# Two-layer cross-attention and expert model on one core: the fullest of the last five second experts is worked last, and the end waits for tiles that hold rows

## The chip, the cores and the metric

The kernel runs on one core of one Trainium2 chip. The metric is the time of one execution on the device, in microseconds (us). Before the change the median of three runs is 881.79 us (879.25 to 882.55).

## The reference

The input is 16 items of 128 rows by 256 features, 2048 rows in all, and a context of the same shape. Two layers follow each other, each an attention over the context and a mixture of experts, both added to the rows with a gain. The part that matters here is the second mixture. Its eight experts are three-layer networks of width 256, 512, 512, 256, and each row goes to the two experts with the highest gate:

```python
gate_logits = jnp.einsum('bsd,dn->bsn', x, Wg) + bg
gate_weights = jax.nn.softmax(gate_logits, axis=-1)
topv, topi = jax.lax.top_k(gate_weights, TOPK)
h = jax.nn.gelu(jnp.einsum('bsd,ndh->nbsh', x, W1) + b1[:, None, None, :], approximate=False)
h = jax.nn.gelu(jnp.einsum('nbsh,nhf->nbsf', h, W2) + b2[:, None, None, :], approximate=False)
eo = jnp.einsum('nbsf,nfd->nbsd', h, W3) + b3[:, None, None, :]
comb = jnp.sum(jax.nn.one_hot(topi, NE, dtype=x.dtype) * topv[..., None], axis=-2)
out = jnp.einsum('nbsd,bsn->bsd', eo, comb)
```

The first mixture has 16 smaller experts and a shared one, and the same routing by two.

## The kernel before, in words

The five engines each have an instruction stream written out by hand; they meet through counting semaphores. The kernel has four stages. Stage A works through the 16 items in groups of four: first attention, shared expert, first routing. Stage B works 47 tiles of 128 rows through the first experts. Stage C (`c_turn` on VectorE, `item_turns`) goes item by item through the second attention and, two items at a time, through the second routing; VectorE keeps in `cnt` how many rows each expert has got so far, computes the slot of each row, and POOL scatters the normalised rows by indirect DMA into `xg1`, one region per expert. The pairs are routed at even turns, the last one (items 14 and 15) at turn 18, and `cnt` then gets its last sum.

`tables` (lines 746 to 821) runs on VectorE once after stage A and once after stage C. From the counts it makes the number of tiles of each expert (at least one for a second expert), their running sum `end`, and for each of the 39 second tiles (`NT1`) a row of `tab`: its expert, its first row in `xg1` and the place of its weights in a ring of three. Tiles past the last with rows get the last expert and the first row of `xg1`, and are computed like the others. It also makes `endi` (the ends, as integers), the two slots of each row in the tile order (`yslot`), sorted so that slot 0 is the lower one, and the number of stores of each parity after which all experts but the last are stored (lines 808 to 810). Before the tiles can be loaded, SP and ScalarE each write zeros behind the rows of four experts (`zero_tails`, lines 300 to 308).

Stage D works the 39 tiles. SP loads a tile into one of four buffers (`load_tile`), TensorE turns it and computes three products in pieces of high and low parts (line 1793), with VectorE splitting each operand (lines 1217, 1219) and ScalarE applying the activation (line 1419). In turn t of `p_turn` TensorE does the third product of tile t-1, the first of tile t+2 and the second of tile t+1. The first product of a tile waits until the weights of its expert are split. VectorE adds the last bias at line 1238, once the store of the tile two places before has landed, and SP stores the tile at line 449 (`store_output`).

POOL brings the weights. `load_weights(e)` issues three DMAs of expert e into one of two raw buffers, and `split_weights(e)` splits them into a place of the ring with a cast (line 509) and a subtraction (line 514), once the expert three before it has no tile left (`endi`). After the last split POOL gathers. 16 indirect DMAs bring the lower slot of each item's rows into the raw buffer of odd experts, after the stores of all tiles of experts 0 to 6; 16 more bring the higher slot into the other buffer, after the stores of all 39 tiles:

```python
stores = pool.value_load(endi[0:1, E1:E1 + 1], min_val=0, max_val=NT1 // 2)
for b in range(2):
    pool.wait_ge(s[f"output_stored{b}"], stores * 16)
```

VectorE, behind its last tile, adds the 16 low rows and then, two items at a time, the high ones (line 1246), and SP, behind its last tile store, stores each pair of finished items (line 462).

Of the kernel before, what the change touches and what calls it, by code (L numbers as in the profile page):

```python
# [54 lines left out]
def flamingo_kernel(nc, x, ctx, g_xattn, g_ffn, theta_wT, theta_b, phi_wT, phi_b, g_wT, g_b, ln_gamma, ln_beta,  # L55
# [26 lines left out]
    with ExitStack() as es:  # L82
# [68 lines left out]
        tab = sb("tab", [1, NT0, 3], I32)  # L151
# [204 lines left out]
        def _(sp):  # L356
# [106 lines left out]
            sp.wait_ge(s["out_stored"], NGE * 16)  # L463


        @blk.gpsimd
        def _(pool):
# [23 lines left out]
            def load_weights(e):  # L491

                at, b = 0, raw_buffer(e)
                for W, k_ in ((W1, KD), (W2, KH), (W3, KH)):
                    size = k_ * W.shape[2]
                    pool.dma_start(raw[b][:, at:at + size].rearrange("p (k n) -> p k n", k=k_),
                                   W[e].rearrange("(k p) n -> p k n", p=P)).then_inc(s[f"raw_loaded{b}"], 16)
                    at += size
# [171 lines left out]
            for b in range(2):  # L670
                pool.wait_ge(s[f"output_stored{b}"], (NT1 + 1 - b) // 2 * 16)
# [7 lines left out]
        def _(dve):  # L679
# [65 lines left out]

            def tables(lk, E, NT):
# [12 lines left out]
                if E == E1:  # L759
# [5 lines left out]
                lk.then(v.tensor_tensor(le, iota_f[:, 0:E].unsqueeze(2).to_broadcast((P, E, E)),  # L765
                                        iota_f[:, 0:E].unsqueeze(1).to_broadcast((P, E, E)), ALU.is_ge))
                lk.then(v.tensor_tensor(le, le, nt.unsqueeze(1).to_broadcast((P, E, E)), ALU.mult))
# [6 lines left out]
                lk.then(v.tensor_reduce(tabf[:, 0:NT, 0], ge, AX, ALU.add))  # L774
                lk.then(v.tensor_scalar(tabf[:, 0:NT, 0], tabf[:, 0:NT, 0], float(E - 1), None, ALU.min))
# [4 lines left out]
                lk.then(v.tensor_scalar(tabf[:, 0:NT, 2], iota_f[:, 0:NT], end[:, E - 1:E], float(P), ALU.is_lt, ALU.mult))  # L780
# [4 lines left out]
                if E == E1:  # L785


                    times = (E1 + 1) // RING
                    over = big1[:, 0:times * NT].rearrange("p (m t) -> p m t", m=times)
                    v.tensor_scalar(tabf[:, 0:NT, 2], tabf[:, 0:NT, 0], 2.0, None, ALU.add)  # L790
                    for m_ in range(times):
                        i = v.tensor_scalar(over[:, m_, :], tabf[:, 0:NT, 0], float(RING * (m_ + 1) - 2), -float(RING), ALU.is_ge, ALU.mult)
# [252 lines left out]
            def c_turn(t, k):  # L1045
# [154 lines left out]
                if choice:  # L1200
                    assert lk.k == PAIR

            item_turns(dve, c_turn)
# [239 lines left out]
        def _(pe):  # L1443
# [443 lines left out]
```

## Time and profile before

| what | value |
|---|---|
| median of three runs | 881.79 us |
| lowest and highest run | 879.25 and 882.55 us |
| the profiled execution | 890.49 us, of which 888.8 us are the span of its records |
| granted TensorE clock over the span | 0.891 of full speed |
| TensorE busy | 705.9 us (79%) |
| VectorE busy | 504.9 us (57%) |
| ScalarE, GpSimd (POOL) busy | 334.3 and 345.8 us (38% and 39%) |

The profile is of one execution; times in it count from the start of its span. PE is TensorE's matmul, PEld its weight load, DVE is VectorE, ACT ScalarE, POOL GpSimd, and SP the engine that issues most DMAs; a q behind a name is its sequencer, which issues DMAs and waits. L1793 is line 1793 of the kernel. A tile name such as `R` or `Q` stands for the memory that several named views share: `wraw` and `R` are the two raw buffers, `Q` holds the input and output tiles of stage D. An arrow reads out<-in. The records of matmuls have modelled ends.

### The profile page before, as it was taken

To read this page: it belongs to the slowest core of one execution; us is meant where nothing else is said; L and a number is where in the kernel's file an instruction comes from. 1 tells how busy PE (TensorE), PEld (TensorE's weight loads), DVE (VectorE), ACT (ScalarE), POOL (GpSimd) and SP (SyncE) were. 2 spreads that over 40 slices of the span, in tenths; PEclk is the share of its full clock that TensorE was granted. 3 is DMA by queue.
4 is the path that set the end of the run, shared out by engine and by line. 5 is a ranking of instruction groups with operands and counts; after the bars stand their busy time and mean duration, and the time that the engine had idled before them with its cause. 6 is when DMAs were issued, how large, how long until landed. Compare 5 with 4: busy or idle time off the path is not lost.

```text
span 888.8 us, 16798 instructions
## 1 busy us (share of the span) xinstructions
PE 705.9 (79%) x3975; PEld 524.9 (59%) x3976; DVE 504.9 (57%) x1347; ACT 334.3 (38%) x861; POOL 345.8 (39%) x355
## 2 busy tenths in 40 slices
PE   4788888835788897888788884499999999999910
PEld 2655665423555545666565662278888888888710
DVE  2547677571233346888788854545555555555533
ACT  0221340301244462455545561144545444454400
POOL 6243544350222233224445333690093448000175
PEclk9958999576899998989999986599999999999955
DMA  8931221033533327877677701543134131110135
GB/s 225 351 115 48 96 70 48 13 135 112 177 118 118 118 72 151 146 130 136 130 149 145 139 32 42 181 150 126 35 125 141 41 130 35 41 35 24 41 115 165
DMA packets 71340, 97.92 MB, mean 110 GB/s; under 512 B 11265, under 2 KB 59745, under 8 KB 71169
## 3 DMA queue, kind: packets, MB, share of 16 engines
q1 hardware_dynamic: 52960, 47.28, 22.2%
q0 software_dynamic: 14944, 47.89, 17.1%
q10 hardware_dynamic: 3392, 2.23, 0.8%
q8 instruction: 20, 0.33, 0.2%
q14 instruction: 24, 0.19, 0.1%
HBM read 63.81 MB, written 33.29 MB: 109 GB/s over the span
## 4 chain that ended last, share of the span: by engine, by line
PE 56%; issue 16%; DMA 9%; DVE 7%; POOL 6%; SPq 3%; ACT 3%; DVEq 0%; POOLq 0%; ACTq 0%
PE ps L1793 23%; PE ps L1624 5%; PE ps L1820 4%; PE ps L1614 3%; PE ps L1695 3%; PE ps L1634 3%; DMA QK<-qscr 2%; PE ps L1544 2%; PE ps L1713 2%; PE ps L1687 2%; POOL R L674 2%; POOL wraw L668 2%; DMA yg<-Q 2%; POOL xg L647 1%; PE ps L1574 1%
## 5 line engine op out<-in xcount | busy, mean ns | idle before, releaser
L1793 PE MATMUL ps<-WR,Hap 128*128 x468 | 118.5, 402 | 3.7 <-DVE Hap L1219 3.7
L1066 DVE TENSOR_REDUCE mraw<-ps 128x2 f32<-128x512 f32 x128 | 86.9, 683 | 22.0 <-PE ps L1687 20.5
L1425 ACT COPY Q<-ps 128x512 f32<-128x512 f32 x78 | 45.7, 586 | 142.3 <-PE ps L1793 142.2
L1793 PEld LDWEIGHTS ps<-WR,Hap 128*128 128x128 f32 x468 | 86.1, 191 | 21.2 <-issue 4.4
L1384 ACT ACTIVATE Q<-ps 128x512 f32<-128x512 f32 x128 | 74.2, 601 | 61.7 <-PE ps L1695 28.2
L1687 PE MATMUL ps<-QK 96*128 96x256 f32 x256 | 62.3, 328 | 21.5 <-DVE mraw L1066 10.1
L1217 DVE CAST Hbp<-ps 128x512 fp32r<-128x512 f32 x39 | 27.0, 692 | 78.6 <-ACT ps L1419 78.6
L1614 PE MATMUL ps<-ident,Q 128*128 128x128 f32 x172 | 36.8, 297 | 43.6 <-DMA Q<-xg 33.6
L1713 PE MATMUL ps<-QK 128*128 128x256 f32 x256 | 64.4, 335 | 7.1 <-ACT Q L1384 4.7
L1793 PE MATMUL ps<-WR,Hbp 128*128 x468 | 66.5, 292 | 2.9 <-issue 2.9
L483 POOL TENSOR_SCALAR veps<-st 128x1 f32<-128x1 f32 (+1 forms) x40 | 10.3, 259 | 138.1 <-DVE st L1108 62.9
L1793 PE MATMUL ps<-WR,XTp 128*128 x234 | 62.7, 404 | 1.3 <-DVE XTp L1219 1.3
L327 POOL DMA_DIRECT2D yg<-Q x46 | 25.0, 543 | 99.1 <-ACT Q L1329 99.1
L1687 PEld LDWEIGHTS ps<-QK 96*128 96x128 f32 x256 | 42.9, 204 | 32.6 <-DVE mraw L1066 16.9
L1793 PEld LDWEIGHTS ps<-WR,Hbp 128*128 128x128 f32 x468 | 59.4, 193 | 3.3 <-issue 3.2
L1614 PEld LDWEIGHTS ps<-ident,Q 128*128 128x128 f32 x172 | 21.4, 146 | 66.9 <-issue 60.5
L1713 PEld LDWEIGHTS ps<-QK 128*128 128x128 f32 x256 | 41.2, 202 | 21.9 <-issue 13.7
L1624 PE MATMUL ps<-R,Q 128*128 x188 | 52.0, 401 | 0.3 <-issue 0.3
L1820 PE MATMUL ps<-ident,Q 128*128 128x128 f32 x312 | 48.5, 278 | 4.1 <-issue 3.7
L668 POOL DMA_INDIRECT wraw<-yg,yslot x16 | 15.4, 963 | 89.9 <-DMA yg<-Q 85.4
L509 POOL CAST WR<-wraw 128x1024 fp32r<-128x1024 f32 (+1 forms) x8 | 18.6, 2319 | 78.7 <-PE ps L1793 69.1
L1793 PEld LDWEIGHTS ps<-WR,XTp 128*128 128x128 f32 x234 | 42.7, 195 | 8.9 <-issue 1.6
(265 smaller groups left out, 1511.5 us busy)
## 6 DMA issues: line engine op xcount, KB each, us to landing
Q<-xg SPq DMA_DIRECT2D x86, 128.0 KB, 2.1
QK<-kscr SPq DMA_DIRECT2D x48, 128.0 KB
QK<-qscr SPq DMA_DIRECT2D x48, 128.0 KB
yg<-Q POOLq DMA_DIRECT2D x47, 128.0 KB, 2.0
wraw<-in_W POOLq DMA_DIRECT2D x10, 512.0 KB, 8.2
wraw<-in_W POOLq DMA_DIRECT2D x5, 1024.0 KB, 7.5
yg<-Q SPq DMA_DIRECT2D x39, 128.0 KB
qscr<-split SPq DMA_DIRECT2D x32, 128.0 KB, 2.1
```

The costliest lines, as they stand in the source:

```text
L668: pool.indirect_dma_start(gLow[:, j, :], None, yg1[:, :], bass.IndirectOffsetOnAxis(ap=yslot[:, j, 0:1], axis=0)).then_inc(s["low_gathered ...
L1066: v.tensor_reduce(mraw[:, b, h, :], ps[:, h % 2, :].rearrange("p (c l) -> p c l", c=2), AX, ALU.max).then_inc(s["s_max"], 1)
L1217: v.tensor_copy(parts[0], src).then_inc(s[copied], 1)
L1384: a.activation(PTb[:, h % 4].rearrange("p c q -> p (c q)"), ps[:, 2 + h % 2, :], ACT.Exp, scale=DH ** -0.5).then_inc(s["st_exp"], 1)
L1425: a.copy(pre, ps[:, bank, :]).then_inc(s[f"l1_h{which}_copied"], 1)
L1614: i = tr(ps[:, b, k * P:(k + 1) * P], Xin[:, x, k * P:(k + 1) * P], ident[:])
L1624: i = mm(ps[:, 2 + b, 0:2 * F0], XTt[:, b, k * P:(k + 1) * P], Wug[:, bass.ds(e, 1), k, :, :].rearrange("p x a f -> p (x a f)"), start=(k ...
L1634: mm(ps[:, 4 + b, 0:D], h0T[:, b, :], Wds[:, bass.ds(e, 1), :].rearrange("p a d -> p (a d)"), start=True, stop=True).then_inc(s["tile_y"], 1)
L1687: i = mm(ps[:, h % 2, c * D:(c + 1) * D], QS[0:NK, n, h, c * P:(c + 1) * P], KS[0:NK, n, h, :], start=True, stop=True)
L1713: i = mm(ps[:, 2 + h % 2, c * D:(c + 1) * D], KS[:, k, h, c * P:(c + 1) * P], QS[:, k, h, :], start=True, stop=True)
L1793: i = mm(out, parts(x_part, k), ring[:, bass.ds(place, 1), o:o + width].rearrange("p r n -> p (r n)"), start=(k == 0 and x_part == 0 and w ...
L1820: i = tr(ps[:, bank, f * P:(f + 1) * P], pre[:, f * P:(f + 1) * P], ident[:])
```

## The change

Three things change. At the end of turn 17 of stage C, when 14 of the 16 items are counted, VectorE computes an order of the second experts (`order_experts`): of experts 3 to 7 the one with most rows so far is moved to the last place, and those behind it move up by one. The tables count places instead of experts where order matters, `tab` gets a fourth column with the place, and POOL reads from `tail` which expert's weights to load for a place from 3 on. Last, the waits of the two rows of gathers: `tables` computes for each parity the number of stores up to the last place but one, and up to the last place, and POOL waits for these, so that the tiles past the last with rows are not waited for by POOL. Their computation and their stores stay.

```diff
@@ sync, at the end
             sp.wait_ge(s["out_stored"], NGE * 16)
+            for b in range(2):
+                sp.wait_ge(s[f"output_stored{b}"], (NT1 + 1 - b) // 2 * 16)
@@ load_weights
                 at, b = 0, raw_buffer(e)
+                which = e if e < RING else pool.value_load(tail[0:1, E1 + e:E1 + e + 1], min_val=0, max_val=E1 - 1)
                 for W, k_ in ((W1, KD), (W2, KH), (W3, KH)):
                     size = k_ * W.shape[2]
                     pool.dma_start(raw[b][:, at:at + size].rearrange("p (k n) -> p k n", k=k_),
-                                   W[e].rearrange("(k p) n -> p k n", p=P)).then_inc(s[f"raw_loaded{b}"], 16)
+                                   W[bass.ds(which, 1)].rearrange("o (k p) n -> p (o k) n", p=P)).then_inc(s[f"raw_loaded{b}"], 16)
@@ gpsimd, after the splits
-            stores = pool.value_load(endi[0:1, E1:E1 + 1], min_val=0, max_val=NT1 // 2)
-            for b in range(2):
-                pool.wait_ge(s[f"output_stored{b}"], stores * 16)
+            def tiles_stored(which):
+                at = E1 + 2 * which
+                stores = [pool.value_load(endi[0:1, at + b:at + b + 1], min_val=0, max_val=(NT1 + 1) // 2) for b in range(2)]
+                for b in range(2):
+                    pool.wait_ge(s[f"output_stored{b}"], stores[b] * 16)
+
+            tiles_stored(0)
             alone(pool)
...
-            for b in range(2):
-                pool.wait_ge(s[f"output_stored{b}"], (NT1 + 1 - b) // 2 * 16)
+            tiles_stored(1)
             alone(pool)
@@ vector, new
+            place_of_e = meta[:, 6, 0:E1]
+            last_e, up_by, down_by, place_end = (meta[:, 8, k:k + 1] for k in range(4))
+            behind, up_to = (r[:, 2:4].rearrange("p j k e -> p (j k e)").rearrange("p (e f) -> p e f", e=E1) for r in (ohx, oh))
+
+            def order_experts(lk):
+                E, n = E1, RING
+                scratch, chosen, ids = meta[:, 5, 0:E], meta[:, 7, 0:E], iota_f[:, 0:E]
+                lk.then(v.tensor_tensor(scratch, cnt[:, 0:E], base[E][:], ALU.subtract))
+                lk.then(v.scalar_tensor_tensor(scratch, scratch, float(2 * E), ids, ALU.mult, ALU.add))
+                lk.then(v.tensor_reduce(place_end, scratch[:, n:E], AX, ALU.max))
+                lk.then(v.tensor_scalar(chosen[:, n:E], scratch[:, n:E], place_end, None, ALU.is_equal))
+                lk.then(v.tensor_tensor(chosen[:, n:E], chosen[:, n:E], ids[:, n:E], ALU.mult))
+                lk.then(v.tensor_reduce(last_e, chosen[:, n:E], AX, ALU.add))
+                lk.mark(v.tensor_scalar(up_by, last_e, -1.0, float(E), ALU.mult, ALU.add))
+                lk.then(v.tensor_scalar(down_by, last_e, float(E), None, ALU.subtract))
+                beyond, moved = meta[:, 0, 0:E], meta[:, 1, 0:E]
+                lk.mark(v.tensor_scalar(beyond, ids, last_e, None, ALU.is_ge))
+                lk.mark(v.tensor_scalar(scratch, ids, last_e, up_by, ALU.is_equal, ALU.mult))
+                lk.then(v.tensor_scalar(chosen, ids, float(E - 1), down_by, ALU.is_equal, ALU.mult))
+                lk.mark(v.tensor_tensor(scratch, scratch, beyond, ALU.subtract))
+                lk.then(v.tensor_tensor(moved, chosen, beyond, ALU.add))
+                lk.mark(v.tensor_tensor(moved, moved, ids, ALU.add))
+                lk.then(v.tensor_tensor(place_of_e, scratch, ids, ALU.add))
+                lk.mark(v.tensor_copy(tail[0:1, E:2 * E], moved[0:1, :]))
+                at = place_of_e.unsqueeze(1).to_broadcast((P, E, E))
+                lk.mark(v.tensor_tensor(behind, place_of_e.unsqueeze(2).to_broadcast((P, E, E)), at, ALU.is_ge))
+                lk.then(v.tensor_tensor(up_to, ids.unsqueeze(2).to_broadcast((P, E, E)), at, ALU.is_ge))
@@ tables, where E == E1
+                    total = place_end
+                    lk.mark(v.tensor_reduce(total, nt, AX, ALU.add))
+                    lk.then(v.tensor_tensor(le, behind, nt.unsqueeze(1).to_broadcast((P, E, E)), ALU.mult))
...
+                    moved = big1[:, NT * E:NT * E + 2 * NT].rearrange("p (m t) -> p m t", m=2)
+                    lk.mark(v.tensor_scalar(moved[:, 0, :], tabf[:, 0:NT, 3], last_e, None, ALU.is_ge))
+                    lk.then(v.tensor_scalar(moved[:, 1, :], tabf[:, 0:NT, 3], float(E - 1), down_by, ALU.is_equal, ALU.mult))
+                    lk.then(v.tensor_tensor(moved[:, 0, :], moved[:, 0, :], moved[:, 1, :], ALU.add))
+                    lk.mark(v.tensor_tensor(tabf[:, 0:NT, 0], tabf[:, 0:NT, 3], moved[:, 0, :], ALU.add))
...
-                lk.then(v.tensor_copy(endi[0:1, 0:E], end[0:1, :]))
-                v.tensor_copy(tab[0:1, 0:NT, :], tabf[0:1, 0:NT, 0:3]).then_inc(s["table_ready"], 1)
+                n_col = 4 if E == E1 else 3
+                if E != E1:
+                    lk.then(v.tensor_copy(endi[0:1, 0:E], end[0:1, :]))
+                v.tensor_copy(tab[0:1, 0:NT, 0:n_col], tabf[0:1, 0:NT, 0:n_col]).then_inc(s["table_ready"], 1)
@@ tables, where E == E1, behind the table
-                    halves = tabf[:, 0:NT // 2, 3]
-                    lk.then(v.tensor_scalar(halves, iota_f[:, 0:NT // 2], 2.0, end[:, E - 2:E - 1], ALU.mult, ALU.is_lt))
-                    lk.then(v.tensor_reduce(meta[:, 5, 0:1], halves, AX, ALU.add))
-                    lk.then(v.tensor_copy(endi[0:1, E:E + 1], meta[0:1, 5, 0:1]))
+                    le = big1[:, 0:E * E].rearrange("p (e f) -> p e f", e=E)
+                    ends = meta[:, 5, 0:E]
+                    lk.then(v.tensor_tensor(le, up_to, nt.unsqueeze(1).to_broadcast((P, E, E)), ALU.mult))
+                    lk.then(v.tensor_reduce(ends, le, AX, ALU.add))
+                    n_half = (NT + 1) // 2
+                    halves = big1[:, 0:2 * n_half].rearrange("p (x i) -> p x i", x=2)
+                    for x in range(2):
+                        i = v.tensor_scalar(halves[:, x, :], iota_f[:, 0:n_half], 2.0, ends[:, E - 2 + x:E - 1 + x], ALU.mult, ALU.is_lt)
+                    lk.then(i)
+                    stores = meta[:, 5, E:E + 4].rearrange("p (x b) -> p x b", x=2)
+                    lk.then(v.tensor_reduce(stores[:, :, 0], halves, AX, ALU.add))
+                    lk.then(v.tensor_tensor(stores[:, :, 1], ends[:, E - 2:E], stores[:, :, 0], ALU.subtract))
+                    lk.then(v.tensor_copy(endi[0:1, 0:E + 4], meta[0:1, 5, 0:E + 4]))
@@ end of c_turn
+                if isinstance(t, int) and t == B + 1:
+                    order_experts(ll)
@@ p_turn
-                    e1, place1 = pe.value_load(tab[0:1, t + 2, 0:1], min_val=0, max_val=E1 - 1), place_of(t + 2)
+                    e1, place1 = pe.value_load(tab[0:1, t + 2, 3:4], min_val=0, max_val=E1 - 1), place_of(t + 2)
```

## Rows read from the trace of the kernel before

**Rows 1.** The page, the chain that ended last, by engine.

```profile
PE 56%; issue 16%; DMA 9%; DVE 7%; POOL 6%; SPq 3%; ACT 3%; DVEq 0%; POOLq 0%; ACTq 0%
```

**Rows 2.** The same chain in order of time, its end: start us, us, what.

```profile
829.60 2.83 PE ps L1793 x18
836.40 2.31 DMA yg<-Q
```

**Rows 3.** Timeline of POOL from 836: start us, us, engine, line, operation, count, idle before.

```profile
839.57 1.02 POOL L668 DMA_INDIRECT wraw<-yg,yslot  x1 [85.35 <-DMA yg<-Q]
...
859.86 0.96 POOL L674 DMA_INDIRECT R<-yg,yslot  x1 [0.31 <-issue]
...
862.38 1.03 POOL L674 DMA_INDIRECT R<-yg,yslot  x1 [0.30 <-issue]
...
865.30 3.26 POOL L674 DMA_INDIRECT R<-yg,yslot  x1 [0.31 <-issue]
...
881.67 0.96 POOL L674 DMA_INDIRECT R<-yg,yslot  x1 [0.30 <-issue]
```

**Rows 4.** Timeline of all engines from 836: VectorE, and TensorE's last product.

```profile
841.11 0.42 DVE L1238 TENSOR_TENSOR Q<-ps,b3bc 128x256 f32<-128x256 f32 x1 [0.15 <-issue]
...
846.81 2.92 PE L1793 MATMUL ps<-WR,Hbp 128*128 x12 [2.92 <-issue]
...
855.59 0.42 DVE L1238 TENSOR_TENSOR Q<-ps,b3bc 128x256 f32<-128x256 f32 x1 [8.38 <-remote]
...
861.30 6.42 DVE L1246 SCALAR_TENSOR_TENSOR xs<-wraw,wts,xs 128x256 f32<-128x256 f32 x16 [5.28 <-DMA wraw<-yg,yslot]
...
884.50 0.88 DVE L1246 SCALAR_TENSOR_TENSOR xs<-R,wts,xs 128x256 f32<-128x256 f32 x2 [1.64 <-DMA R<-yg,yslot]
```

**Rows 5.** Timeline of SP: the stores of tiles 26, 36 and 38.

```profile
776.18 0.36 SPq L449 DMA_DIRECT2D yg<-Q  x1
...
841.62 0.33 SPq L449 DMA_DIRECT2D yg<-Q  x1
...
856.11 0.33 SPq L449 DMA_DIRECT2D yg<-Q  x1
```

**Rows 6.** Timeline: POOL's splits for places 6 and 7, TensorE's first products of tiles 26, 27.

```profile
731.45 9.03 POOL L514 TENSOR_TENSOR WR<-R,WR 128x4096 fp32r<-128x4096 f32 x1 [0.18 <-POOL WR L509]
...
745.17 9.04 POOL L514 TENSOR_TENSOR WR<-wraw,WR 128x4096 fp32r<-128x4096 f32 x1 [0.18 <-POOL WR L509]
...
748.25 1.55 PE L1793 MATMUL ps<-WR,XTp 128*128 x6
...
755.00 1.55 PE L1793 MATMUL ps<-WR,XTp 128*128 x6
```

**Rows 7.** Timeline of VectorE: the last gate, the table, the slots, the first tile's cast.

```profile
549.44 0.17 DVE L1162 TENSOR_REDUCE lmx<-lb 128x2 f32<-128x16 f32 x1
549.65 0.17 DVE L1172 TENSOR_TENSOR ex<-lb,lmx 128x16 f32<-128x16 f32 x1
...
550.10 0.17 DVE L1076 TENSOR_REDUCE den<-ex 128x2 f32<-128x16 f32 x1 [0.28 <-ACT ex L1407]
...
561.13 0.27 DVE L797 CAST tab<-tabf 1x117 int32<-1x117 f32 x1
...
564.92 0.18 DVE L821 CAST yslot<-idxf 128x32 uint32<-128x32 f32 x1
...
566.03 0.42 DVE L1217 CAST XTp<-ps 128x256 fp32r<-128x256 f32 x1 [0.92 <-PE ps L1614]
```

**Rows 8.** The chain in order of time: the last zeroed tail and the first loaded tile.

```profile
560.56 1.70 DMA xg<-zeros
563.07 2.06 DMA Q<-xg
```

**Rows 9.** Windows: stretch, its length, busy us (count) of each engine, clock, DMA share, GB/s.

```profile
842.00:844.00 2.00, 1.89 (x17) 1.65 (x15) 0.00 (x0) 0.59 (x1) 1.49 (x2) 1.00 0.52 141
...
846.00:848.00 2.00, 1.19 (x5) 1.19 (x6) 1.08 (x2) 0.00 (x0) 1.70 (x2) 0.51 0.40 109
```

More of the change, by code:

```diff
@@ L150, in flamingo_kernel @@
         tabf = sb("tabf", [P, NT0, 4])
-        tab = sb("tab", [1, NT0, 3], I32)
+        tab = sb("tab", [1, NT0, 4], I32)
         endi = sb("endi", [1, E0], I32)
@@ L764, in tables @@
                 le = big1[:, 0:E * E].rearrange("p (e f) -> p e f", e=E)
-                lk.then(v.tensor_tensor(le, iota_f[:, 0:E].unsqueeze(2).to_broadcast((P, E, E)),
-                                        iota_f[:, 0:E].unsqueeze(1).to_broadcast((P, E, E)), ALU.is_ge))
-                lk.then(v.tensor_tensor(le, le, nt.unsqueeze(1).to_broadcast((P, E, E)), ALU.mult))
+                total = end[:, E - 1:E]
+                if E == E1:
+                    total = place_end
+                    lk.mark(v.tensor_reduce(total, nt, AX, ALU.add))
+                    lk.then(v.tensor_tensor(le, behind, nt.unsqueeze(1).to_broadcast((P, E, E)), ALU.mult))
+                else:
+                    lk.then(v.tensor_tensor(le, iota_f[:, 0:E].unsqueeze(2).to_broadcast((P, E, E)),
+                                            iota_f[:, 0:E].unsqueeze(1).to_broadcast((P, E, E)), ALU.is_ge))
+                    lk.then(v.tensor_tensor(le, le, nt.unsqueeze(1).to_broadcast((P, E, E)), ALU.mult))
                 lk.then(v.tensor_reduce(end, le, AX, ALU.add))
@@ L773, in tables @@
                                         end.unsqueeze(1).to_broadcast((P, NT, E)), ALU.is_ge))
-                lk.then(v.tensor_reduce(tabf[:, 0:NT, 0], ge, AX, ALU.add))
-                lk.then(v.tensor_scalar(tabf[:, 0:NT, 0], tabf[:, 0:NT, 0], float(E - 1), None, ALU.min))
+                at = 3 if E == E1 else 0
+                lk.then(v.tensor_reduce(tabf[:, 0:NT, at], ge, AX, ALU.add))
+                lk.then(v.tensor_scalar(tabf[:, 0:NT, at], tabf[:, 0:NT, at], float(E - 1), None, ALU.min))
+                if E == E1:
+                    moved = big1[:, NT * E:NT * E + 2 * NT].rearrange("p (m t) -> p m t", m=2)
[3 more added lines that the diff above has]
+                    lk.mark(v.tensor_tensor(tabf[:, 0:NT, 0], tabf[:, 0:NT, 3], moved[:, 0, :], ALU.add))
                 lk.then(v.tensor_tensor(ge, ge, nt.unsqueeze(1).to_broadcast((P, NT, E)), ALU.mult))
@@ L778, in tables @@
                 lk.then(v.tensor_tensor(tabf[:, 0:NT, 1], iota_f[:, 0:NT], tabf[:, 0:NT, 1], ALU.subtract))
-                lk.then(v.tensor_scalar(tabf[:, 0:NT, 2], iota_f[:, 0:NT], end[:, E - 1:E], float(P), ALU.is_lt, ALU.mult))
+                lk.then(v.tensor_scalar(tabf[:, 0:NT, 2], iota_f[:, 0:NT], total, float(P), ALU.is_lt, ALU.mult))
                 lk.then(v.tensor_tensor(tabf[:, 0:NT, 1], tabf[:, 0:NT, 1], tabf[:, 0:NT, 2], ALU.mult))
@@ L789, in tables @@
                     over = big1[:, 0:times * NT].rearrange("p (m t) -> p m t", m=times)
-                    v.tensor_scalar(tabf[:, 0:NT, 2], tabf[:, 0:NT, 0], 2.0, None, ALU.add)
+                    v.tensor_scalar(tabf[:, 0:NT, 2], tabf[:, 0:NT, 3], 2.0, None, ALU.add)
                     for m_ in range(times):
-                        i = v.tensor_scalar(over[:, m_, :], tabf[:, 0:NT, 0], float(RING * (m_ + 1) - 2), -float(RING), ALU.is_ge, ALU.mult)
+                        i = v.tensor_scalar(over[:, m_, :], tabf[:, 0:NT, 3], float(RING * (m_ + 1) - 2), -float(RING), ALU.is_ge, ALU.mult)
                     lk.then(i)
@@ L1201, in c_turn @@
                     assert lk.k == PAIR
+                if isinstance(t, int) and t == B + 1:
+                    order_experts(ll)
+            ll.before = NGA * LATE
+            ll.turn(0, 0)
             item_turns(dve, c_turn)
```

## The prediction

> **What bounds the kernel now.** I read the chain that ended last first. Over the whole span it is mostly TensorE [rows 1]; in order of time TensorE carries it through the tiles of the second experts until 836 us, then it passes to the store of one tile [rows 2] and to POOL. The reader should see what POOL does there: after 85 us of idleness it issues 32 indirect gathers, one every 1.26 us, from 839.57 to 882.63 [rows 3]. The next view, the timeline of the same stretch, shows what stands beside them: VectorE writes the output of tile 36 at 841.11 and of tile 38, the last, at 855.59, then adds the 16 low rows in 6.42 us from 861.30, and finishes the last high pair 0.88 us after 884.50 [rows 4]. So after 839.57 us the end is set by POOL's issue of gathers, not by tiles. The low gathers start there because they wait for the store of tile 35: experts 0 to 6 end at place 36. Running the reference's router over its inputs gives rows per expert 1077, 24, 797, 492, 8, 1205, 439, 54, that is 9, 1, 7, 4, 1, 10, 4, 1 tiles, 37 in all; tiles 37 and 38 are empty.
>
> **What the change removes.** Among experts 3 to 7 expert 5 has most rows, by so much that the two items not yet counted can't alter it. The order becomes 0, 1, 2, 3, 4, 6, 7, 5 and the places end at 9, 10, 17, 21, 22, 26, 27, 37 tiles. A token's lower slot then lies before tile 27, so the 16 low gathers wait for the store of tile 26, issued at 776.18 [rows 5], and end near 779.3 + 20.2 = 799.5 us, while tiles 29 and 30 run. That is the gain: 16 gathers, 859.86 - 839.57 = 20.3 us [rows 3], leave the chain.
>
> **What takes their place.** The high gathers now wait for the store of tile 36, not of 38. It is issued at 841.62 [rows 5]; a store lands in 2.31 us [rows 2], POOL starts 0.8 us later as it did at 839.57, so at 844.7 us. Sixteen gathers at 1.26 us end at 864.6 if nothing disturbs them. VectorE can't start its low adds before it has written tile 38, at 856.0 [rows 4], because they stand behind it in its queue. They then run from 856.0 to 862.4, beside the gathers. In the trace the three gathers begun from 862.38 to 865.30, beside such adds, took until 868.56, 6.2 us instead of 3.5 [rows 3]: 2.7 us lost. After the change the adds of high rows already gathered follow at once, so VectorE is busy for about 10.5 us without a break (6.4 for 16 low rows, some 4 for nine or ten high ones), against 8 in the trace. I take 3.7 us of loss; the ends are 2.7 and 4.7. The last gather ends at 864.6 + 3.7 = 868.3. From there to the end of the span the trace has 888.8 - 882.6 = 6.2 us (landing, last pair, last store). New end without costs: 874.5, a saving of 14.3 us. If the gathers lost nothing, VectorE itself would end its adds at 856.0 + 6.4 + 16 x 0.44 = 869.4, and 3.4 us of stores give 872.8; with 4.7 us it is 875.5. SP is no term: it stores tile 38 at about 856, before the first pair of rows is ready.
>
> The lock deserves a check. While VectorE added, three gathers were slowed, but they were not stopped for all of the 6.42 us [rows 3, 4].
>
> The Trainium skill (SBUF — State Buffer, Who interferes with whom) has VectorE and GpSimd share a port pair, and whichever comes second is blocked fully. By that rule the gathers could stand still for the whole burst of adds; the trace agrees in part only, with one gather of 3.26 us.
>
> **What the change adds.** (a) The order is computed on VectorE at the end of the turn before the last pair is routed: 18 small operations, 11 of them waited for. A small one steps by 0.21 us (549.44 to 549.65) [rows 7], so 11 x 0.21 = 2.3 for the waited ones, and an estimated half of that for each of the seven that are not, 0.7: 3.0 us. VectorE has only 0.3 us of idleness there, before 550.10 [rows 7]. Everything behind is a chain: the last pair's routing, the tails, the tables, the first tile. I charge 2.8 us, with ends 2.0 (some operations fall closer together) and 3.6. (b) The tables grow. Up to the table itself: four operations on 39 elements and a sum are added, a mask and a copy are removed, net 0.4 us. The table is ready at 561.4 [rows 7], but SP waits for the zeroed tails (560.56 + 1.70 = 562.26) and loads at 563.07 [rows 8]: covered; were that cover gone, it would cost 0.4. From the table to the slots: seven operations and a copy in place of three, about 0.8 us. VectorE is free 1.2 us later, at 566.3 instead of 565.1, and the first cast of a tile began at 566.03 [rows 7]: 0.3 us on the path. POOL's first split moves by 1.2 us too; its result is wanted nine tiles later, so nothing. (c) Register work: POOL reads one value for each of five weight loads, in a queue that idles for tens of microseconds between splits; TensorE, VectorE and SP read as many as before. Nothing.
>
> **(d) The weights' order.** This is where cover could fail. Place 7 is now needed for tile 27, not for tile 36. Its split can't start earlier, as the place whose buffer it takes still ends at tile 22: POOL finishes it at 745.17 + 9.04 = 754.21, and TensorE starts tile 27's first product at 755.00 [rows 6]. A margin of 0.8 us, so zero; each microsecond beyond costs one. Place 6 (split ended at 740.5) is wanted at 748.3: safe. I allow 0 to 1.5 us.
>
> **The sum**, against the profiled execution (890.49 us, of which 888.8 are span): -14.3 + 2.8 + 0.3 = -11.2 us. The median of the runs is 881.79, 8.7 below that execution, with runs from 879.25 to 882.55; I carry the difference over unscaled: 870.6 us. With the ends (872.8 or 875.5 for the tail, 2.3 or 5.4 of cost) the change lies between -13.7 and -7.9, so 868.1 to 873.9, and 1.5 us each way for the scatter of runs.
>
> **Rivals.**
> - **The adds stop the gathers.** If the port is held for the whole burst, POOL stands for 6.4 us and for each high row's add that is ready behind it, some nine, 3.8 us: 10.2 us lost instead of 3.7, so 870.6 + 6.5 = 877.1 us. For it: the 3.26 us gather. Against: gathers got through in that burst. By the Trainium skill's rule above the time would be this one. 8%.
> - **The end still waits for all tiles**, because the count of tiles with rows isn't what reaches POOL. Then the high gathers start after tile 38's store (issued 856.1 [rows 5], landed and seen 3.1 later), at 859.2, as now at 859.86: nothing gained, 2 to 3 us of cost, near 884 us. The arithmetic of the diff speaks against it. 3%.
> - **Slower: the low gathers hold up the tiles they now run beside.** Place: the wait of VectorE for the tile store two places back, and the products it feeds. For it: with the gathers running, tile 38's output came only after 8.4 us of idleness [rows 4], though TensorE began its last product at 846.81. If each of three tiles lost 6 us so, it would be 18 us, and 888.6 in all. It decides from 5.2 us a tile, (11.2 + 4.4) / 3. Against: from 842 to 844, with gathers moving 141 GB/s, TensorE was busy 1.89 of 2.00 us at full clock, and the slow output falls where the granted clock is 0.51, after a drained pipeline [rows 9]. 4%.
> - **A late place 7.** POOL's split is slowed or begun later; TensorE idles, and its clock may fall. 2 to 4 us, 873 to 875. 8%; it overlaps the main case's range.
>
> **How the numbers follow.** Main case 77%: 870.6, own range 866.6 to 875. The rivals have 8, 3, 4 and 8%. The range 866.5 to 877.3 takes in the late place and the lock and leaves out the two others and the tails. A measurement of this kernel can tell about 0.5%, 4.4 us, from no change: below 877.4 counts as faster. Main case, late place and a part of the lock (its 877.1 lies at the edge) give 0.87; the rest of it and the wait for all tiles, 0.08; the held-up tiles, 0.05.
>
> **What would show it.** Sixteen gathers into the first buffer near 779 to 800 us (plus the shift of 3), with TensorE's products at their old pace beside them; the second sixteen from some 4 us after tile 36's output, while the last tiles still run; a block of small VectorE operations of about 3 us after the gate of the last pair; POOL's last split ending just before tile 27's first product. The forecast is wrong if the low gathers appear only after tile 35, if the high ones start after tile 38's store, if TensorE waits at tile 27, or if a gap opens between the tiles at 780 to 805 us.

## The result, and the profile after

The change makes the kernel slower, by 1.0%. The kernel after has a median of 892.68 us (883.49 to 896.09, 5 runs), the kernel before 881.79 us (878.5 to 884.74, 5 runs of the same session): ratio 1.0097, 95% interval 1.0055 to 1.014. The forecast was 870.6 us. All ratios in this document leave out runs in the slow state (one of four of e4_extra, one of seven of e6_narrow, five of the 25 of before beside e1 to e4); the medians include them.

The profiled execution after took 883.49 us (span 881.9). It and that of before differ by 13 us before the changed code runs: the last gate's first operation is at 549.23 us before and at 536.09 after, a stretch whose length varies from run to run. So the two are compared from that operation on. From it to the end of the span: before 888.8 - 549.2 = 339.6 us, after 881.9 - 536.1 = 345.8 us, that is 6.2 more. In three stretches:

```
stretch                                          before   after    forecast
last gate to tile 0's first product               17.94    20.90    +3.1
tile 0's first product to tile 38's first        263.70   280.52     0
tile 38's first product to the end                57.93    44.39   -14.3
```

The first stretch is +2.96, the third -13.5: both as forecast. The middle one was to stay as it was and grew by 16.8 us.

The page of after, the chain that ended last, by engine (to [rows 1]):

```profile
PE 58%; DVE 12%; issue 9%; DMA 8%; POOL 4%; ACT 3%; another core or an unknown queue 2%; SPq 2%; DVEq 0%; POOLq 0%; ACTq 0%
```

POOL's share falls from 6 to 4%: the low gathers left the chain. "Another core or an unknown queue", 2% on a kernel of one core, is new. It is time for which the profile names no releaser: 16.64 and 1.68 us near 771 and 788 us, where the time went, and 2.89 us at 409.54, in the routing, beside a row of four scatters (406.65 to 411.58). Two of these pieces and the end of the same chain in order of time, start us, us, what (to [rows 2]):

```profile
771.27 16.64 another core or an unknown queue
...
788.46 1.68 another core or an unknown queue
...
847.76 0.43 DVE Q L1306
...
848.27 3.33 DMA yg<-Q
...
852.48 0.95 POOL R L681
...
859.23 3.65 POOL R L681
...
874.76 2.93 DMA R<-yg,yslot
```

Its end now runs through tile 36's output and store, as the change intends, and through 16 gathers, not 32. The timeline of POOL after, start us, us, engine, line, operation, count, idle before (to [rows 3] and [rows 6]):

```profile
733.60 9.02 POOL L517 TENSOR_TENSOR WR<-wraw,WR 128x4096 fp32r<-128x4096 f32 x1 [0.18 <-POOL WR L512]
767.25 1.02 POOL L676 DMA_INDIRECT wraw<-yg,yslot  x1 [24.62 <-DMA yg<-Q]
...
786.25 0.96 POOL L676 DMA_INDIRECT wraw<-yg,yslot  x1 [0.30 <-issue]
852.48 0.95 POOL L681 DMA_INDIRECT R<-yg,yslot  x1 [65.27 <-DMA yg<-Q]
```

The 16 low gathers go out in one row without a pause, one every 1.26 us, from 767.25 to 787.21. Now the timeline of TensorE in the same stretch:

```profile
743.37 1.55 PE L1861 MATMUL ps<-WR,XTp 128*128 x6
...
771.10 1.55 PE L1861 MATMUL ps<-WR,XTp 128*128 x6
...
773.06 3.01 PE L1861 MATMUL ps<-WR,Hap 128*128 x12
788.58 1.11 PE L1888 MATMUL ps<-ident,Q 128*128 128x128 f32 x4 [12.51 <-ACT Q L1493]
793.04 2.92 PE L1861 MATMUL ps<-WR,Hbp 128*128 x12 [3.35 <-DVE Hbp L1287]
795.76 2.38 PE L1861 MATMUL ps<-WR,XTp 128*128 x6
```

Tile 27's first product (743.37) comes 0.75 us after POOL's split for place 7 (733.60 + 9.02): in time. Tile 31 starts at 771.10, tile 32 only at 795.76, 24.66 us later, where a tile takes 6.7 to 7.4. TensorE waits for ScalarE and VectorE; what do they wait for? The timelines of ScalarE and VectorE:

```profile
787.94 0.58 ACT L1493 COPY Q<-ps 128x512 f32<-128x512 f32 x1 [16.66 <-remote]
```

```profile
772.03 0.69 DVE L1287 TENSOR_TENSOR Hap<-ps,Hap 128x512 fp32r<-128x512 f32 x1
791.47 0.69 DVE L1285 CAST Hbp<-ps 128x512 fp32r<-128x512 f32 x1 [18.75 <-ACT ps L1487]
```

The circle starts at ScalarE's copy at 787.94. It copies what TensorE's first products of tile 31 wrote, and by the modelled ends those were over at 772.65. "Remote" says that the profile found no releaser near the end of the wait. The trace file also holds the moment at which each semaphore is raised (no view prints it), and there the delay shows. XTp, Hap and Hbp are what the first, second and third product of a tile read:

```
product that signals                     modelled end   signal   late by
after: Hbp products just ahead of tile 31   771.26      779.44     8.18
after: first products of tile 31 (XTp)      772.65      787.91    15.27
after: the Hap products behind them         776.07      790.26    14.19
before: last products of tile 38 (Hbp)      849.74      855.46     5.72
```

ScalarE is released 0.03 us after the signal of 787.91, and that signal comes 0.7 us after the last gather's end at 787.21. The fourth row was in the trace of before all along: the 8.4 us of idleness ahead of tile 38's output [rows 4] end 0.13 us after this signal, with the low gathers under way beside it.

Were the products themselves late, or only their signals? The transposes that stand between those first products and the Hap products (modelled end 773.30) signal at 790.13, and the twelve Hap products behind them only 0.13 us later, at 790.26. The same two signals are 2.77 us apart where nothing is held (798.81 and 801.58). So most of the twelve products had run before the signal ahead of them was raised. The same pair comes 0.12 to 0.13 us apart in e4_extra, e6_narrow and e11_three_flying below. For the first products of tile 31 this can't be told.

Windows of the stretch: stretch, its length, busy us (count) of TensorE, its weight loads, VectorE, ScalarE, POOL, clock, DMA share, GB/s; after first, then e2_pairs, an experiment described below, in which nothing is held:

```profile
764.00:771.50 7.50, 7.50 (x47) 6.49 (x47) 4.46 (x9) 3.84 (x12) 3.34 (x4) 1.00 0.24 70
771.50:779.00 7.50, 4.57 (x23) 3.45 (x22) 1.19 (x2) 0.00 (x0) 5.67 (x7) 1.00 0.41 122
779.00:788.00 9.00, 0.00 (x0) 0.00 (x0) 0.00 (x0) 0.06 (x1) 6.38 (x7) 0.58 0.36 104
788.00:795.80 7.80, 3.87 (x17) 3.48 (x18) 3.65 (x7) 3.16 (x10) 0.00 (x0) 0.50 0.12 37
```

```profile
771.50:779.00 7.50, 7.50 (x45) 6.37 (x44) 3.94 (x7) 4.19 (x14) 3.91 (x4) 1.00 0.29 86
779.00:788.00 9.00, 8.63 (x49) 6.82 (x47) 5.66 (x11) 4.05 (x13) 1.94 (x3) 1.00 0.27 89
```

All engines but POOL fall silent together, and the DMA engines are at 0.36 to 0.41 of their time, so no transfer path is full on average. The granted clock falls from full to half (2.4 to 1.2 GHz) at 780.5, after TensorE's last recorded product has ended (776.07): so it can't be what stopped it. It stays at half until 797.6 and costs a little of what comes at 788 to 796.

The timeline of VectorE after, at the last gate and the tables (to [rows 7]) and at the end (to [rows 4]):

```profile
536.50 0.17 DVE L1236 TENSOR_TENSOR ex<-lb,lmx 128x16 f32<-128x16 f32 x1
536.59 0.16 DVE L763 TENSOR_TENSOR meta<-cnt,base 128x8 f32<-128x8 f32 x1
...
539.46 0.21 DVE L782 TENSOR_TENSOR oh<-iota_f,meta 128x64 f32<-128x64 f32 x1
539.70 0.17 DVE L1140 TENSOR_REDUCE den<-ex 128x2 f32<-128x16 f32 x1
...
555.76 0.18 DVE L885 CAST yslot<-idxf 128x32 uint32<-128x32 f32 x1
555.85 0.42 DVE L1285 CAST XTp<-ps 128x256 fp32r<-128x256 f32 x1
```

```profile
855.30 0.42 DVE L1306 TENSOR_TENSOR Q<-ps,b3bc 128x256 f32<-128x256 f32 x1 [1.42 <-issue]
855.64 6.42 DVE L1314 SCALAR_TENSOR_TENSOR xs<-wraw,wts,xs 128x256 f32<-128x256 f32 x16
862.09 1.67 DVE L1314 SCALAR_TENSOR_TENSOR xs<-R,wts,xs 128x256 f32<-128x256 f32 x4
...
877.72 0.88 DVE L1314 SCALAR_TENSOR_TENSOR xs<-R,wts,xs 128x256 f32<-128x256 f32 x2 [1.67 <-DMA R<-yg,yslot]
```

The order of the experts is worked out from 536.59 to 539.67, and den, the gate's next step, stands at 539.70, 3.20 us after ex where it was 0.45 us before: 2.75 for the order, against 2.8 charged.

### The profile page after: what moved, and what is told of

The parts are those of the page before. It is cut to its first block, busy times and chain, and to the rows that moved or that the text cites. A ratio compares the mean times of both kernels' runs of the same rounds, so it can differ in the third digit from the quotient of the medians.

```text
span 881.9 us, 16879 instructions
## 1 busy us (share of the span) xinstructions
PE 700.3 (79%) x3975; PEld 519.0 (59%) x3976; DVE 508.1 (58%) x1372; ACT 333.2 (38%) x861; POOL 347.7 (39%) x355
## 4 chain that ended last, share of the span: by engine, by line
PE 58%; DVE 12%; issue 9%; DMA 8%; POOL 4%; ACT 3%; another core or an unknown queue 2%; SPq 2%; DVEq 0%; POOLq 0%; ACTq 0%
PE ps L1861 24%; PE ps L1692 5%; PE ps L1888 4%; PE ps L1682 3%; PE ps L1702 3%; PE ps L1573 2%; PE ps L1763 2%; PE ps L1755 2%; PE ps L1642 2%; POOL R L681 2%; PE ps L1781 2%; DMA yg<-Q 2%; DVE mraw L1130 2%; PE ps L1612 1%
## 5 line engine op out<-in xcount | busy, mean ns | idle before, releaser
L1888 PE MATMUL ps<-ident,Q 128*128 128x128 f32 x312 | 48.9, 280 | 16.8 <-ACT Q L1493 12.8
L1682 PEld LDWEIGHTS ps<-ident,Q 128*128 128x128 f32 x172 | 21.3, 145 | 59.6 <-issue 53.7
L1888 PEld LDWEIGHTS ps<-ident,Q 128*128 128x128 f32 x312 | 35.4, 142 | 30.2 <-issue 15.9
```

The costliest lines, as they stand in the source:

```text
L1682: i = tr(ps[:, b, k * P:(k + 1) * P], Xin[:, x, k * P:(k + 1) * P], ident[:])
L1888: i = tr(ps[:, bank, f * P:(f + 1) * P], pre[:, f * P:(f + 1) * P], ident[:])
```

## The experiments

Two theories were set against each other first: a row of indirect gathers holds TensorE (its signals come late while POOL issues them), or something else in the change opens the gap. Diffs are against the kernel after, but for e4_extra.

**e1_low_late**: the low gathers wait for tile 35's store, as before the change (both semaphores at 18 stores); order, tables and the second wait stay changed.

```diff
             tiles_stored(0)
+            for b in range(2):
+                pool.wait_ge(s[f"output_stored{b}"], 18 * 16)
             alone(pool)
```

> The changed kernel with the new order kept, but its low gathers held until tile 35 is stored, as before the change. Theory G (indirect gathers hold TensorE back while POOL issues them): no gap between the first products of tiles 31 and 32, which are then 6.8 us apart instead of 24.7; the end as before the change, so 882 + 3 us of ordering = 885. Rival O (the new order itself stalls the tiles, by late weights): the gap of 18 us stays and the time is near 900.

Measured: 890.22 us (median of 10), ratio 1.0078 (1.0034 to 1.0122). The gap is gone: tile 32 starts 6.79 us after tile 31. So order and tables do not make the gap. But the time is not that of before plus 3. The timelines of VectorE, TensorE and POOL of e1_low_late near its end:

```profile
864.03 0.42 DVE L1308 TENSOR_TENSOR Q<-ps,b3bc 128x256 f32<-128x256 f32 x1 [14.51 <-remote]
```

```profile
849.11 2.92 PE L1863 MATMUL ps<-WR,Hbp 128*128 x12 [3.87 <-issue]
```

```profile
840.42 1.02 POOL L678 DMA_INDIRECT wraw<-yg,yslot  x1 [84.59 <-DMA yg<-Q]
...
860.71 0.95 POOL L683 DMA_INDIRECT R<-yg,yslot  x1 [0.30 <-issue]
861.96 0.96 POOL L683 DMA_INDIRECT R<-yg,yslot  x1 [0.31 <-issue]
```

The high gathers follow at 0.30 us, as they did before (859.86 [rows 3]), so the row is 32 long in both. Tile 38's last product (modelled end 852.03) signals at 863.89, 11.9 us late, and the low adds wait for that output. From tile 38's first product to the end it is 60.2 us, 57.9 before: the gain of the second part is eaten by a longer hold, which I had not expected. Why it is 11.9 us here and 5.7 before is not shown; here the signal came when the row still had 18 us to go.

**e2_pairs**: the low gathers go two at a time, each two behind the output of one more tile, from tile 26 on.

```diff
             for j in range(B):
+                if j % 2 == 0:
+                    pool.wait_ge(s["tile_out"], NT0 + 27 + j // 2)
+                    alone(pool)
                 pool.indirect_dma_start(gLow[:, j, :], None, yg1[:, :],
```

> The changed kernel with its 16 low gathers issued two at a time, one pair behind the output of each of tiles 26 to 33. If theory G holds in proportion (each gather costs TensorE about 1.1 us wherever it stands), the time stays near 892, with some 2 us lost in each of eight tiles. If TensorE is held only after several gathers on end (in the traces the delay set in 3 to 4 us after the first one), the tiles keep their 6.8 us and the time is 871 to 875.

Measured: 873.09 us (median of 10), ratio 0.9918 (0.9874 to 0.9962). The timeline of POOL of e2_pairs:

```profile
773.45 1.00 POOL L679 DMA_INDIRECT wraw<-yg,yslot  x1 [0.30 <-issue]
776.81 0.95 POOL L679 DMA_INDIRECT wraw<-yg,yslot  x1 [2.35 <-DVE Q L1309]
...
783.43 0.96 POOL L679 DMA_INDIRECT wraw<-yg,yslot  x1 [4.41 <-DVE Q L1309]
```

The same 16 gathers of the same rows, with tile steps of 6.7 to 7.4 us beside them. From the last gate to the end it takes 868.7 - 540.6 = 328.1 us, 11.5 less than before; my sum was -11.2. But 1.6 of the 11.5 is half clock in the trace of before, at 576 us, and not of the change: 9.9 are left, and the ratio's interval stands for 3.4 to 11.1. So most of the prediction's sum comes back once the row is broken up, and this kernel is faster than both.

**e3_plain**: in place of each low gather a plain transfer of as many bytes in the same queue.

```diff
-                pool.indirect_dma_start(gLow[:, j, :], None, yg1[:, :],
-                                        bass.IndirectOffsetOnAxis(ap=yslot[:, j, 0:1], axis=0)).then_inc(s["low_gathered"], 16)
+                pool.dma_start(gLow[:, j, :], yg1[j * P:(j + 1) * P, :]).then_inc(s["low_gathered"], 16)
```

> The changed kernel with 16 plain DMAs of 128 KB on POOL's queue in place of the 16 low gathers, from the first 16 tiles of the result; the low rows that are added are then others than the reference's. Rival T (traffic: 2 MB moved in a burst beside the tiles is what holds TensorE): the gap at tile 32 stays, 10 us or more. Theory G (it is the indirect form): no gap, time 870 to 876.

Measured: 871.5 us (median of 8), ratio 0.9899 (0.9848 to 0.995); tile 32 comes 6.87 us after tile 31. POOL issues the sixteen in 8.52 us, faster than the indirect ones, and holds nobody. Their row is shorter than 20 us, but eight indirect gathers in 9.9 us do hold TensorE (e9_eights below). Neither the bytes, nor the destination, nor a busy queue of POOL's is enough; the indirect form matters.

**e4_extra**: the kernel before, with 16 indirect gathers more (of other rows, into the same buffer, which the true gathers then overwrite) behind tile 26's store.

```diff
+            for b in range(2):
+                pool.wait_ge(s[f"output_stored{b}"], (14 - b) * 16)
+            alone(pool)
+            for j in range(B):
+                pool.indirect_dma_start(gLow[:, j, :], None, kscr.rearrange("a t d -> (a t) d"),
+                                        bass.IndirectOffsetOnAxis(ap=slotl[:, j % GA, j // 8:j // 8 + 1], axis=0)).then_inc(s["extra"], 16)
+            pool.wait_ge(s["extra"], B * 16)
...
+                    few = big1[:, 0:2 * GA].rearrange("p (j k) -> p j k", j=GA)
+                    lk.then(v.tensor_scalar(few, slotf[:, 0:GA, :], float(2 * TOK - 1), None, ALU.min))
+                    v.tensor_copy(slotl[:], few)
```

> The kernel before with 16 more indirect gathers, from another tensor into the first raw buffer, behind the store of tile 26; nothing of the change in it. Theory G: a gap of 15 to 20 us opens between the first products of tiles near 31, and the time is 897 to 904. Rival O: POOL is idle there, so nothing: 882 to 883.

Measured: 902.03 us (median of 4), ratio 1.0234 (1.0131 to 1.0338). Tile 32 comes 24.59 us after tile 31, and the wait is the known one, though the view puts it down to "issue" here. The timeline of ScalarE of e4_extra (its gathers went from 762.53 to 782.5):

```profile
780.41 0.58 ACT L1435 COPY Q<-ps 128x512 f32<-128x512 f32 x1 [13.82 <-issue]
785.53 1.11 ACT L1429 ACTIVATE ps<-ps,b2T 128x128 f32<-128x128 f32 x4 [4.53 <-remote]
```

So the hold needs nothing of the change: the row alone, put beside tiles of the old kernel, makes it.

**e5_fours**: as e2_pairs, in rows of four behind every second tile (the condition is `j % 4 == 0`).

> The changed kernel with its low gathers issued four at a time (5 us on end), every second tile. Theory G with an onset (TensorE is held only from about 3.5 us after the first of a row of gathers, until the row ends): about 1.5 us lost in each of four rows, gaps of 8 to 9 us between some first products of tiles 28 to 36, and a time of 876 to 880. If the loss is one for the row of sixteen alone, 873 as in pairs.

Measured: 872.29 us (median of 4), ratio 0.9875 (0.9822 to 0.9929). Four tile steps are a little long: 7.03, 7.37, 7.74 and 7.27 us where e2_pairs has 6.79, 6.75, 6.81 and 6.66, 2.4 us in all. The 876 to 880 us of the theory with an onset at 3.5 us were too much.

**e6_narrow**: each low gather moves 64 columns, a quarter of the bytes.

```diff
-                pool.indirect_dma_start(gLow[:, j, :], None, yg1[:, :],
+                pool.indirect_dma_start(gLow[:, j, 0:D // 4], None, yg1.rearrange("t (a d) -> (t a) d", a=4),
```

> The changed kernel with each low gather fetching a quarter of each row (64 columns, 256 bytes; as many indices and gathers on end as before, and a quarter of the bytes); the low rows that are added are wrong in all columns. If the issue of indirect gathers (indices and descriptors) is what holds TensorE: the gap of 18 us at tile 32 stays, 890. If it is their data: a gap of 5 us or less, 873 to 878.

Measured: 891.93 us (median of 7), ratio 1.0077 (1.0034 to 1.0121). The gap stays, 24.39 us from tile 31 to tile 32. A quarter of the data holds TensorE as long, so it is not the bytes. The first products' signal (modelled end 784.43) comes at 796.69, 2.2 us before the row ends at 798.93: the hold does not last exactly as long as the row.

**e7_pairs_all**: as e2_pairs, but the high gathers wait for all 39 tiles, as before the change.

```diff
-            tiles_stored(1)
+            for b in range(2):
+                pool.wait_ge(s[f"output_stored{b}"], (NT1 + 1 - b) // 2 * 16)
```

> The low gathers in pairs, and the high gathers waiting for the stores of all 39 tiles, as before the change. It prices the second part of the change. Both theories: in pairs the high gathers began 4.7 us behind the store of tile 36; with the wait they begin behind that of tile 38, some 10 us later, so 873 + 10 = 883, less 2 to 3 us since VectorE's low adds are then over before most of the gathers: 879 to 883.

Measured: 881.1 us (median of 10), ratio 0.9966 (0.9931 to 1.0001). From tile 38's first product to the end it is 50.5 us, 45.0 in e2_pairs: in the traces the second part of the change is worth 5.5 us (8.0 by the medians of two sessions), and its high gathers start at 853.3. A time at the middle of what was expected, and no difference from before that can be told. So without the second part no gain can be told, and the second part without the earlier low gathers (e1_low_late) gained nothing either.

**e8_landed**: each low gather waits until the one before has landed.

```diff
+                if j > 0:
+                    pool.wait_ge(s["low_gathered"], j * 16)
+                    alone(pool)
```

> The changed kernel with each low gather waiting until the one before has landed, so that one at a time is under way, about one every 2.7 to 3 us, 45 us in all beside the tiles. If it takes gathers issued on end, or several outstanding, to hold TensorE: no gap, 870 to 875. If each gather costs TensorE about 1 us whenever it runs: 2 to 3 us more in each of seven tiles, 888 to 892.

Measured: 870.69 us (median of 2), ratio 0.9861 (0.9776 to 0.9945). One gather every 3.5 us, no gap.

**e9_eights**: as e2_pairs, in two rows of eight (`j % 8 == 0`).

> The changed kernel with its low gathers in two rows of eight, four tiles apart. Rows of two cost nothing, rows of four some 0.5 us each, the row of sixteen 18 us. If the loss grows with what a row has beyond about 3.5 us: a row of eight is 10 us long and costs 6 us, 12 in all, 883 to 887. If TensorE's late product only has to wait until the row is over: each row costs what is left of it when a product is caught, 3 to 7 us.

Measured: 890.33 us (median of 2), ratio 1.0103 (0.9985 to 1.0222). Two runs say little by their time; the trace does: each row of 9.8 to 9.9 us costs one tile step 7.0 or 7.1 us (13.83 and 13.96 where 6.8 is usual). With the other lengths:

```
gathers in the row      2      4            8            16
length of the row, us   2.2    4.9          9.9          20.0
tile time lost, us      0.0    0.2 to 0.9   7.0, 7.1     17.8
```

From eight on, the loss is the row's length less 2 to 3 us. It is no fixed price for each gather: sixteen in pairs cost nothing.

**e10_two_flying** and **e11_three_flying**: at most two, or three, gathers under way at once. Each gather signals `done`, and VectorE's low adds wait for all of them. Two, then three:

```diff
+                done = s["extra" if j % 2 else "low_gathered"]
+                if j > 1:
+                    pool.wait_ge(done, j // 2 * 16)
+                    alone(pool)
...
```

```diff
+                done = s[("low_gathered", "extra", "high_gathered7")[j % 3]]
+                if j > 2:
+                    pool.wait_ge(done, j // 3 * 16)
+                    alone(pool)
...
```

> The changed kernel with each low gather waiting until the last but one has landed, so that at most two are outstanding; one about every 1.8 to 2 us, 30 us in all. If what holds TensorE is gathers piling up (three or four outstanding): no gap, 871 to 875. If it is a row without a pause on POOL, there are short pauses here too, and the gap is gone or small as well; if instead it is the rate of gathers, with more than one per 3 us: a gap of 5 to 15 us, 877 to 887.

> The changed kernel with at most three low gathers outstanding. A gather lands some 3.2 us after its issue begins, so POOL then issues one every 1.3 us, almost as in the unlimited row of sixteen, only nothing can pile up. If what holds TensorE is a pile of outstanding gathers: no gap, 870 to 874. If it is the rate or the lack of pauses: a gap of 10 to 18 us at tile 32 or so, 882 to 892.

Measured: with two 869.65 us (median of 2), ratio 0.9868 (0.9756 to 0.9981), no gap; with three 889.39 us (median of 2), ratio 1.0115 (0.9913 to 1.0318, too wide to say by itself), but with a gap of 24.43 us in its trace. The timelines of POOL, of e10_two_flying and of e11_three_flying:

```profile
778.99 0.95 POOL L680 DMA_INDIRECT wraw<-yg,yslot  x1 [1.26 <-DMA wraw<-yg,yslot]
...
782.80 0.95 POOL L680 DMA_INDIRECT wraw<-yg,yslot  x1 [1.58 <-DMA wraw<-yg,yslot]
```

```profile
784.75 0.96 POOL L680 DMA_INDIRECT wraw<-yg,yslot  x1 [0.33 <-issue]
786.01 0.96 POOL L680 DMA_INDIRECT wraw<-yg,yslot  x1 [0.30 <-issue]
```

A cap of three hardly delays POOL (0.33 for 0.30 us), since by the fourth gather the first has landed: three under way are no pile, and the hold is whole. A cap of two makes pauses of 1.3 to 1.6 us. That leaves the pause, or the count of two, as what helps.

**e12_pauses**: no wait for any landing, but a memset of 0.97 us between each two gathers and the next.

```diff
+                if j % 2 == 0 and j > 0:
+                    nc.gpsimd.memset(gC[:], 0.0).then_inc(s["pool_a"], 1)
+                    pool.wait_ge(s["pool_a"], 5 + j // 2)
+                    alone(pool)
```

> The changed kernel with a memset of 1024 columns (about 1 us) on POOL between each two low gathers, and no wait for any landing. If a pause of 1 us and more after each two suffices, however many are outstanding: no gap, 870 to 874. If the outstanding gathers count, which nothing limits here: gathers every 1.9 us leave two outstanding at most times, so the gap may go as well, and then this run only says that the rate of 1.9 us is harmless; a gap of several us would say that landings have to be waited for.

Measured: 874.42 us (median of 6), ratio 0.991 (0.9855 to 0.9965), tile steps of 6.6 to 7.5 us as usual. The timeline of POOL of e12_pauses:

```profile
778.16 1.00 POOL L680 DMA_INDIRECT wraw<-yg,yslot  x1 [0.30 <-issue]
779.17 0.97 POOL L677 MEMSET gC<- 128x1024 f32 x1
780.95 0.96 POOL L680 DMA_INDIRECT wraw<-yg,yslot  x1 [0.81 <-POOL gC L677]
```

POOL is busy in between, and the row of gathers pauses for 1.8 us: that is enough, with no wait for a landing. The count isn't excluded by it: with a pair every 4.0 us and a landing within some 3.5 (the spacing of e8_landed), no more than two were under way here either.

## Why the prediction was wrong

- **The tail** (-14.3) was right: -13.5 measured. Its parts stand too. The high gathers began 4.7 us after tile 36's output, not 3.6: the store took 3.33 us to land, not 2.31. The last gather ended at 875.7, 23.2 us after the first began, so 3.4 us were lost to the adds (16 gathers at 1.26 us take 19.9), where I took 3.7. From there to the end it was 6.2 us, as before.
- **The adds stop the gathers** (8%) did not come. One gather took 3.65 us beside the adds, the others stayed at 0.95 to 1.28. The Trainium skill (SBUF — State Buffer, Who interferes with whom) has whoever comes second at the shared port pair blocked in full; the trace agrees for at most one gather in sixteen.
- **The order and the tables** (+3.1) were right: +2.96. The first cast stands right behind the slots' (555.85 behind 555.76), as forecast.
- **Place 7** (margin 0.8 us) was right: 0.75 us. **The end waits for all tiles** (3%) did not come either.
- **The step that failed** is the sentence that the low gathers "leave the chain" while tiles run, at no cost. It should have carried some 18 us. The rival "the low gathers hold up the tiles they now run beside" had the right stretch and nearly the right size, 18 us and 888.6 in all, at 4%; but its mechanism, the wait for a store two places back, is not what happened, and its size was luck: three tiles at 6 us each, against one gap of 17.8. TensorE's signals came late. The prediction also let the gathers end "while tiles 29 and 30 run"; 20.2 us are three tile steps, with the first products of tiles 31 to 33 (782.73 to 796.95 in the trace of before), so more was exposed to them than it said.

Why did I put it at 4%? Two readings failed. I took the window from 842 to 844 us, with TensorE busy at full clock beside gathers, as evidence against it. But it lay only 2.4 to 4.4 us behind the row's first gather at 839.57, and a row of four (4.9 us) hardly costs anything; after, the records show TensorE busy for another 8.8 us once the row has begun at 767.25. A window further into the row was needed. And I put the 8.38 us ahead of tile 38's output [rows 4] down to the half clock [rows 9]. The granted clock had fallen at 846.05, before that product began; but even at half speed the last product, begun at 846.81, was recorded as over at 849.74, so 5.7 us had no owner, and the row itself says so: "remote".

More evidence lay in the trace of before, where the routing scatters rows with four indirect DMAs in a row. The timelines of POOL, TensorE and VectorE of before:

```profile
419.03 1.10 POOL L647 DMA_INDIRECT xg<-R,slotu  x1 [1.96 <-DVE slotu L1199]
...
422.99 0.96 POOL L647 DMA_INDIRECT xg<-R,slotu  x1 [0.30 <-issue]
```

```profile
421.59 0.50 PE L1687 MATMUL ps<-QK 96*128 96x256 f32 x2
```

```profile
424.81 0.69 DVE L1066 TENSOR_REDUCE mraw<-ps 128x2 f32<-128x512 f32 x1 [2.00 <-PE ps L1687]
```

VectorE reduces these products one by one, and its 61st of 128 reductions, the one shown, reads the 61st product, over at 422.09 by the modelled ends. It was signalled at 424.79, 2.7 us late and 0.8 us after the last of the four scatters ended.

In one sum, from the last gate: +2.96 for order and tables, +18.4 for the held tiles (17.8 at tile 32, 0.6 at tile 34), -13.5 for the tail, and -1.6 that is not of the change (before had 3.4 us of half clock at 576 us, after had none there): +6.2 us. The medians say +10.9, with 4.8 to 12.3 in the ratio's interval. I can't say whether the rest is scatter.

**What is shown and what is not.** Shown: the hold needs the indirect form (e3_plain); it does not need the bytes (e6_narrow), nor more than three under way (e11_three_flying), nor anything else of the change (e4_extra); and it is gone with pauses of 1.3 us or more after each two (e10_two_flying, e12_pauses). Open: what in the chip is held; what ends the hold, as the signal that ScalarE waits for comes 0.7 us after the row's end in the kernel after and 2.2 us before it in e6_narrow, and the one that VectorE waits for in e1_low_late 18 us before it; and whether the pauses help by themselves or by keeping no more than two under way; e5_fours, with three under way inside a row and small losses, speaks for the row's length. Of most of the Hap products it is shown that they had run before the signal ahead of them; whether the first held products ran late or only their signals can't be told, because the ends in the trace are modelled. Whether pauses after three or four gathers, or shorter pauses, would do was not tried.

## What to carry to other kernels

Work that is "hidden beside" a busy engine is free only if that engine has been seen to run on beside as much of it: look for the longest stretch in which both run, not for the first two microseconds of it. Issue indirect gathers in twos with a pause between them (1.3 us was the shortest tried), for instance behind a semaphore that ticks with the tiles; the same sixteen gathers then cost the tiles nothing instead of 17.8 us. And a wait put down as "remote" on a kernel of one core, or a reader that starts long after the modelled end of the product it reads, is a finding, to be explained before any forecast is made of that stretch. The chain of the kernel after shows it twice: at 409.54, beside a row of four, and at 771.27.

## What the runs showed of the hardware

- A row of indirect DMAs that POOL issues on end delays what TensorE signals: by 15.3 us in the kernel after, 11.9 in e1_low_late, 5.7 before. The Trainium skill (SBUF — State Buffer, Who interferes with whom) says "PE and ACT never wait on anyone" and has DMA never contend with a compute engine. The trace here doesn't agree, as a guide to time, though no run tells whether memory ports have a part in it: TensorE had no product in 9 us, beside gathers that write no buffer it uses.
- Sixteen plain transfers of POOL's, issued in 8.52 us, and POOL's arithmetic of 9 us at a time [rows 6] do nothing of the kind: the tile steps beside them are 6.7 to 7.4 us.
- A hold costs only what waits for it. In the trace of before it delayed tile 38's output by some 6 us and cost nothing, because VectorE's low adds waited another 5.28 us for the gathers [rows 4]. Beside tiles that follow each other, the same row is paid nearly in full.
